# Graph attention and a top-2 expert layer on one core: ranks and table offsets of the early token groups earlier, GpSimd's queue in another order

## The reference

```python
h = layernorm(x) @ W.T + b_W
e = (h @ a1)[:, None] + (h @ a2)[None, :] + b_a[0]
e = where(e > 0, e, 0.2 * e)
attention = softmax(where(adj > 0, e, -9e15), axis=1)
x = x + attention @ h
xf = layernorm(x)
topk_logits, topk_idx = top_k(xf @ Wr + br, 2)
gates = softmax(topk_logits)
for e in range(64):
    out += combine[:, e:e+1] * (relu(xf @ W1[e] + b1[e]) @ W2[e] + b2[e])
x = x + out
```

## Time and profile before

| | |
|---|---|
| median of 3 runs | 266.3 us (266.24 to 267.46) |
| the profiled execution | 266.82 us, span 265.1 us |
| busy of the span | PE 222.3 us, DVE 210.0 us, ACT 182.7 us, POOL 155.5 us |
| attention and routing | from 0 to about 151 us of the span |
| expert stage | from about 151 us to the end |

### The profile page before, as it was taken

The page is one execution under the profiler, slowest core; times in us unless marked ns, Lnnn a source line. Parts: engine busy times, 40 slices in busy tenths (PEclk is TensorE's granted clock), DMA queues, the critical chain, the costliest instruction groups (busy, mean ns, idle before and its releaser), DMA issues.

```text
span 265.1 us, 6251 instructions
## 1 busy us (share of the span) xinstructions
PE 222.3 (84%) x1863; PEld 212.4 (80%) x1863; DVE 210.0 (79%) x596; ACT 182.7 (69%) x434; POOL 155.5 (59%) x195
## 2 busy tenths in 40 slices
PE   1493999999996999889946469999999999999840
PEld 1353999999996999789925369999999999999730
DVE  6899999999999989999586117888886666676365
ACT  2758979999876889695635238778767777777400
POOL 5780000533578838688787563446888888865600
PEclk9999599999998999999995559999999999999995
DMA  5989764497757861139811132222369410100067
GB/s 150 225 153 172 139 116 82 129 260 200 206 145 133 282 219 80 43 113 422 357 44 53 35 102 62 63 67 66 83 231 305 154 42 31 40 27 30 24 209 276
DMA packets 11120, 36.89 MB, mean 139 GB/s; under 512 B 2256, under 2 KB 2832, under 8 KB 10320
## 3 DMA queue, kind: packets, MB, share of 16 engines
q0 software_dynamic: 5232, 14.98, 24.7%
q1 hardware_dynamic: 5424, 21.11, 23.1%
q10 hardware_dynamic: 432, 0.40, 0.5%
HBM read 39.36 MB, written 5.51 MB: 169 GB/s over the span
## 4 chain that ended last, share of the span: by engine, by line
PE 61%; DVE 21%; DMA 7%; issue 4%; POOL 3%; SPq 1%; ACT 1%; POOLq 0%; DVEq 0%
PE bank L1157 17%; PE bank L1169 16%; PE bank L1050 13%; PE bank L1026 9%; DVE arena L760 5%; DVE arena L754 4%; DMA xs<-in_x 2%; DMA arena<-result 2%; POOL table L432 2%; PE bank L1146 2%; DVE arena L745 1%; PE bank L1069 1%; DVE idx L784 1%; DVE hot L790 1%; DMA rows_in<-table,arena 1%
## 5 line engine op out<-in xcount | busy, mean ns | idle before, releaser
L1050 PE MATMUL bank<-arena 128*128 128x130 f32 x512 | 62.2, 278 | 0.0
L1157 PE MATMUL bank<-arena 128*128 x384 | 60.5, 282 | 0.1
L1050 PEld LDWEIGHTS bank<-arena 128*128 128x128 f32 x512 | 60.3, 194 | 0.2 <-DVE xs L768 0.2
L1169 PE MATMUL bank<-w2s,arena 128*128 x384 | 58.8, 276 | 0.2 <-issue 0.2
L1157 PEld LDWEIGHTS bank<-arena 128*128 128x128 f32 x384 | 51.6, 196 | 0.6 <-issue 0.3
L1169 PEld LDWEIGHTS bank<-w2s,arena 128*128 128x128 f32 x384 | 50.6, 192 | 0.6 <-issue 0.6
L918 DVE SCALAR_TENSOR_TENSOR arena<-bank,arena 128x128 f32 x96 | 33.6, 350 | 21.5 <-PE bank L1169 20.2
L661 ACT ACTIVATE arena<-bank,arena 128x128 f32<-128x128 f32 x96 | 35.2, 367 | 18.3 <-PE bank L1157 16.9
L432 POOL DMA_INDIRECT table<-rows_in,pos x32 | 40.1, 1254 | 10.0 <-issue 8.0
L1026 PE MATMUL bank<-ident,arena 128*128 128x128 f32 x256 | 34.2, 291 | 9.5 <-DVE arena L760 9.5
L911 DVE TENSOR_SCALAR arena<-bank,arena 128x128 f32<-128x128 f32 x96 | 33.3, 346 | 10.1 <-PE bank L1157 9.9
(11 more groups left out here) (196 smaller groups left out, 278.2 us busy)
## 6 DMA issues: line engine op xcount, KB each, us to landing
arena<-in_adj POOLq DMA_DIRECT2D x16, 512.0 KB, 6.6
w2s<-in_w SPq DMA_DIRECT2D x8, 768.0 KB, 4.5
arena<-in_w SPq DMA_DIRECT2D x6, 1024.0 KB
arena<-in_w SPq DMA_DIRECT2D x4, 512.0 KB, 5.3
w2s<-in_w SPq DMA_DIRECT2D x4, 512.0 KB, 3.9
xs<-in_x SPq DMA_DIRECT2D x4, 256.0 KB, 6.3
arena<-result SPq DMA_DIRECT2D x2, 512.0 KB, 4.3
arena<-result SPq DMA_DIRECT2D x4, 256.0 KB, 5.9
```

What stands on the lines that cost most here:

```text
L1050: ins = pe.matmul(OB[t % 2][:, 0:D + 2], pt_r[:, t % 2, j, :], h[:, j, :], start=(j == 0), stop=(j == T - 1))
L1157: ins = pe.matmul(hp(p, b), w1u[:, p % UW, P * b:P * b + P], xT_all[:, bass.ds(column, P)], start=True, stop=True)
L1169: ins = pe.matmul(yp(p), hT[:, p % UH, b, :], w2s[:, bass.ds(u, 1), b, :].rearrange("p e d -> p (e d)"), start=(b == 0), stop=(b == HB - 1))
```

## The change

No work is added or removed; instructions of three engines take other places in their queues.

```diff
-    PLACED = [(0, 0, 10), (0, 1, 11), (0, 2, 12), (0, 3, 13), (1, 4, 14), (1, 5, 15), (1, 6, 15), (1, 7, 15)]
+    PLACED = [(0, 0, 10), (0, 1, 11), (0, 2, 12), (0, 3, 12), (1, 4, 13), (1, 5, 13), (1, 6, 15), (1, 7, 15)]
...
                 for q in range(COUNTED):
-                    if s == LAST[q] + 5:
+                    if s == LAST[q] + 6:
                         counts(q)
+            place(2, 8)
             rstd_of(6)
-            place(2, 8)
+            place(2, 9)
             rstd_of(7)
-            place(2, 9)
             place(3, 10)
+            place(3, 11)
             rstd_of(8)
-            place(3, 11)
...
                 if s >= 3:
                     residual(s - 3)
+                for q in range(EARLY):
+                    if s == LAST[q] + 6 and s < T - 1:
+                        place(q)
                 leaky(s - 1)
                 for q in range(EARLY):
                     if s == LAST[q] + 5:
                         top2(q)
-                    if s == LAST[q] + 6 and s < T - 1:
-                        place(q)
-            leaky(T - 1)
             residual(T - 3)
             place(2)
+            leaky(T - 1)
...
                 turn(s)
-                attend(s)
-                for q in range(EARLY):
+                for q in range(COUNTED):
                     if s == LAST[q] + 4:
                         route_c(q)
+                attend(s)
+                if s == T - 3:
+                    route_c(2)
```

## The result

The changed kernel takes 269.62 us (median of 5 runs, 267.86 to 269.86), against 266.24 us (5 runs, 265.85 to 267.46) for the kernel before on the same chip. The ratio is 1.0097, 95% interval [1.0059, 1.0134]: it is slower by about 1%, some 2.6 us by the ratio (the two medians are 3.4 us apart). The profiled execution took 267.86 us for a span of 266.1, the fastest of its five; before it was 266.82 for 265.1.

What follows compares the result with a forecast made beforehand. The instant GpSimd reaches the padding scatter was taken to bound the kernel: two fewer scatters behind a later `rstd_of(5)` gave +1.5 us, agreeing with ScalarE's +1.4. So 266.3 + 1.5 = 267.8 us, range 265.0 to 269.3.

Steps and rivals of the forecast that it cites:

- The chain: GpSimd from tile 4's first scatter at 103.7 us: holds by VectorE's passes make `rstd_of(5)` late, padding scatter at 149.65.
- Its opening term: VectorE ahead of `top2(1)`: the shift at step 9 saves most of a 0.64 us wait, taken as 0.5 us.
- The inference of the Trainium skill: GpSimd scatters would run beside VectorE's L760 unheld; given 2 of the sooner rival's 20%, with 263.6 us.
- ScalarE's limit: First evacuation of a gathered tile: work ahead moves +4.1 us, less its 2.66 us wait, gives +1.4 us.
- The size: Padding scatter on GpSimd moves from 148.17 to 149.65 us, so the whole time grows by 1.5 us.
- All behind it I take as unchanged: Everything after GpSimd reaches the padding scatter, including the expert stage, was assumed to keep its length.
- GpSimd's queue. This is what I take to decide: Held scatters and `counts(1)` delay `rstd_of(5)` by 6.3 us, and the padding scatter by 1.5 us.
- turn(12) costs 0 to 1.6 us on TensorE, and at 117 us this is overtaken by the next item either way: `turn(12)` after a gap of some 2.4 us may run at low clock; GpSimd's queue was taken to outweigh it.
- The sooner rival: GpSimd gets through step 13 sooner, `rstd_of(5)` ends by 114.7: -1.2 us, 265.1 us; chance 20%.

Runs made afterwards that it cites:

- the second: The changed kernel run and profiled again with no edit: 269.55 us, ratio 1.0096 to the kernel before.
- +1.8% alone: The kernel before with only GpSimd's queue (scatters, counts, tail) as changed, VectorE and TensorE as before: 271.24 us, ratio 1.0178.
- VectorE and TensorE alone: The changed kernel with GpSimd's three edits undone: 269.69 us, ratio 1.0119 to the kernel before.
- the kernel with the counts ahead: The changed kernel with `counts(1)` one step earlier, ahead of group 1's scatters: 268.01 us, ratio 1.0029 to the kernel before.
- short filler: `counts(1)` early as above, plus eight unused fp32 products on TensorE in each gap ahead of `turn(8)` and `turn(12)`: 266.51 us, ratio 0.9985.
- the last rows of the table: Five runs with `counts(1)` early, plus `deviation(11)` ahead of tile 14's scores, eight unused TensorE products, or both; one with the tail's old order: ratios 0.9975 to 1.0039.
- the old tail order: `counts(1)` early and `deviation(11)` ahead of tile 14's scores, with GpSimd's tail ordered as before the change: 267.15 us, ratio 1.0039.

## Why the prediction was right, and where it wasn't

Point by point, forecast and profile of the changed kernel:

- `pos` of group 1 ready at 103.4: it ended at 102.93. The first scatter held to 106.5: 106.09. Third free at 109.0 to 110.0: 108.55 to 109.52. Fourth held until 112.3: 111.84. `counts(1)` done at 116.3: 115.76. `rstd_of(5)` at 119.2: 118.81. `norm(10)` at 119.25: 118.84. `evac(14)` at 123.7: 123.03. `norm(12)` at 129.65: 129.33. Padding at 149.65: 149.55. The chain held link by link, each instant 0.1 to 0.7 us sooner than worked out.
- *Its opening term.* I took 0.5 us for what the shift at step 9 saves on VectorE. It was 0.8 at `top2(1)` (L779 at 94.54 instead of 95.34), of which only 0.37 is its wait (0.27 us instead of 0.64) and the rest was there at `leaky(11)` before it (91.93 instead of 92.37). It was 1.0 at the L754 behind `leaky(12)` (105.11 instead of 106.09); that is why all instants came a little early.
- *The inference of the Trainium skill* ("SBUF — State Buffer", section "Who interferes with whom") that writing descriptors needs only the write interface, from which a scatter would run beside L760: the rows above speak against it again, with scatters of 2.87 us beside L760 and 0.97 us alone. The time of 263.6 us didn't come.
- *ScalarE's limit* of +1.4: L656 at 156.53 has no wait left, where it had 2.66. The work ahead of it moved by 4.5 us (L669 at 155.60 instead of 151.07), not 4.1, so this limit came out at +1.9. TensorE's first take is at 155.60 instead of 153.97, +1.6, so the two limits met within some 0.3 us.
- *The size*, +1.5 us, is right for what the term measures, the padding scatter: +1.38 in the first profile, +1.89 in the second. It is too small for the time: the ratio of 1.0097 is +2.6 us, and the measured median of 269.62 lies 0.3 us above the top of my range (by the ratio, 266.3 times 1.0097 is 268.9, within it but 1.1 above the forecast). The step that failed is "All behind it I take as unchanged", and with it TensorE's clock, which I priced at `turn(12)` alone. From the first take to the end of the span it is 110.5 us in the first profile (266.1 less 155.60), 111.7 in the second (267.8 less 156.12), and 111.1 before. So the stage isn't longer in every execution of the changed kernel. But seven of its twelve runs have a mean clock that only one of 81 runs of the kernel before has, and the one of the seven that was profiled lost 0.5 us ahead of the padding scatter and 0.6 at the start of the expert stage by it, against the first profile. The rest of the excess stays open.
- *The cause*, "GpSimd's queue. This is what I take to decide", is half of it. It is sufficient (+1.8% alone). But the step "turn(12) costs 0 to 1.6 us on TensorE, and at 117 us this is overtaken by the next item either way" looked at 117 us and not at 113, where the input of `rstd_of(5)` has to be there before VectorE's next pass begins. With the queue undone, `turn(12)` alone costs 1.2% (VectorE and TensorE alone), at 0.50 granted from 106 to 108 us. That it is the clock that decides was seen in the kernel with the counts ahead (short filler); with GpSimd's old queue it wasn't tried. In the changed kernel the one hides behind the other.
- *The sooner rival* had its point of decision right: `rstd_of(5)` ends by 114.7. Where an edit to the changed kernel brought that about, in the five profiles of the last rows of the table (112.36 to 114.76), the padding scatter began at 146.48 to 147.30. That is 0.9 to 1.7 us sooner than before, where I had said 1.2. The time followed only in part: the ratios of these kernels are 0.9975 to 0.9994, a gain of 0.2 to 0.7 us, and with the old tail order, where padding began at 146.97, it is 1.0039. That part stays open; it lies behind the padding scatter.

## What to carry to other kernels

In this kernel a small instruction on GpSimd that others wait for gets through quickly only between two long passes on VectorE: look whether both its queue and its input are there before the next pass begins, and with room for all of its instructions. When a move makes it late for two reasons, undoing one can show nothing, as undoing all of GpSimd's edits did here; undo both. Moving 2 us of work ahead of a producer's pass made a gap of 2 to 3 us on TensorE behind it, and the price of that gap can be the clock of the work after it rather than the gap. A late instruction can make such a gap too, two engines further on. When times of one kernel fall into groups, lay the mean granted clock of each run beside them.

## What the runs showed of the hardware

- Small GpSimd instructions are held by a VectorE pass like scatters are: `rstd` (L414, 128x2) took 0.73 us between passes, and 2.49 to 2.82 us when it met one. A first addition of `counts` took 0.32 us and two together 0.69 alone (`counts(0)` in the changed kernel), and two took 3.11 beside L754.
- The clock after a gap isn't the same from run to run of one program: ahead of `turn(8)`, TensorE had no work for 2.40 us in the first profile of the changed kernel and for 2.20 in the second; the transposes then took 2.61 us and 1.97, at a clock that fell to 0.50 by 79 us in the one and stayed at 1.00 in the other. Ahead of `turn(12)` the gap of 2.87 us gave 2.67 in the kernel with the counts ahead, and the gap of 2.86 in the changed kernel's second profile gave 1.97; the granted clock from 106 to 108 us was 0.62 and 1.00.
- Executions of one program differ from early on: the third L760 started between 35.08 and 36.36 us in the profiles of this study. Where two kernels are compared above, the difference was still there at 102 us (102.48 against 103.00, and 102.27 against 102.94), so padding scatters are to be compared less it. It needn't last: the two profiles of the changed kernel, 35.93 and 35.67 there, have L760 at 102.85 and 102.86. So whether it takes 0.3 us of the changed kernel's +1.38 (35.93 against 35.59) is open.
- Eight fp32 products of 128x128 took 1.95 us, so 0.24 us for one, and the profile counts each as two; a transpose of the same size takes half of that (16 in 1.97).
